# Fills, output projection and input split in smaller pieces at new steps, and the whole rotation on VectorE

## The chip, the core and the metric

The kernel runs on one core of a Trainium2 chip. The metric is the device time of one execution in microseconds (us). Five engines work side by side, each on its own list of instructions, and wait for one another on semaphores: TensorE (PE in the profile; PEld is its weight load), VectorE (DVE), ScalarE (ACT), GpSimd (POOL) and SyncE (SP), which issues most of the transfers between HBM and SBUF.

## The reference, cut to what matters

One transformer layer on 8 sequences ("batches") of 512 rows and 512 columns: differential attention, then a mixture of 8 experts, each with a residual and a layer norm.

```python
q, k, v = x @ Wq, x @ Wk, x @ Wv        # 16 heads of q, 4 of k and v, each two halves of 32 columns
q1, q2, k1, k2 = rope(...)              # o1 = x1*cos - x2*sin ; o2 = x1*sin + x2*cos
a1 = softmax(q1 @ k1.T * scale + mask); a2 = softmax(q2 @ k2.T * scale + mask)
out = (a1 - lam * a2) @ v
out = group_norm(out) * gn_w + gn_b     # mean and variance per head over all 512 rows
x1 = layernorm(x + out * (1 - LAMBDA_INIT) @ Wo)
# then: router, the best 2 of 8 experts for each row, silu(x@wg)*(x@wu)@wd, weighted sum, residual, layernorm
```

## The kernel before

The program has three parts: the attention of all batches, the experts, and the combination of their rows. The change touches the attention alone.

**The steps.** A batch is 48 steps: 4 groups of kv heads, each of 12 units. A unit is a tile of 128 query rows (tile 0 to 3) with two heads (tiles 0 and 1) or one head (tiles 2 and 3). In step s, TensorE computes the scores of unit s (`S<-kT,qT` and the mask), transposes the mixed probabilities of unit s-3 (`PTp<-ident,mixed`), and in some steps multiplies by the values (`O<-probsT,vals`). VectorE takes the row maximum of unit s (`neg_max`), inverts the sums of unit s-1 (`rsum`), mixes the two halves of unit s-2 (`mixed`) and computes the ratio of unit s-1 (`rho`). ScalarE copies the transposed probabilities of unit s-3 and takes the exponentials of unit s (`expd`). S has two buffers, so the scores of step s+1 wait for the exponentials of step s-1. The steps here are counted from the start of `neg_max`.

**The fills.** Beside its steps every batch projects 12 groups of 128 columns (`SEQ`: 8 of q, 2 of k, 2 of v), the first 7 for itself and the last 5 for the next batch. One such group is a fill: 12 matmuls (24 narrower ones for v) into `prep`. `STARTS` gives the step of a fill; half of it runs at the end of that step, half early in the next. For q and k a fill is followed by the rotation: VectorE reads `prep` and writes `turned` (times cos) and `swapped` (neighbours exchanged) one step after the start (`rotate`, L858 to L864), GpSimd multiplies `swapped` by sin and adds it to `turned` (`rope`, L486 to L492), VectorE rounds `turned` to the high part two steps later (`high_part`, L871), and GpSimd subtracts that for the low part (`low_part`, L494 to L498). SyncE stores both parts and loads them again in the layout of the scores (`spread`).

**The tail.** While batch b runs its steps, the tail of batch b-1 runs in them: statistics of the context (`chunk_stats`), group norm factors, 8 normalisations on ScalarE (`norm`, two in each of steps 12 to 15), 32 output projections on TensorE (`oproj`, two in each of steps 16 to 31), the residual and its statistics (`resid`), layer norm, transposition, router logits and the choice of experts. `TAIL_PE` and the tables `mine` of the engines give the steps. The single PSUM bank `tail` passes from task to task.

**The input.** After fill 6 SyncE loads x of the next batch, transposed, into `xl`; ScalarE rounds it to `xh` in step 31 (2048 columns at once), VectorE replaces `xl` by the remainder in step 32, and fill 7 waits for that in step 33.

The order on each engine is written out by hand in those tables; there is no scheduler. A waiting instruction holds everything behind it on its engine. Batches 1 to 6 run in a loop of two bodies; batch 0 has no tail, batch 7 only 7 fills, and its own tail comes after it, alone.

Of the kernel before, what the change touches and what calls it, by code (L numbers as in the profile page):

```python
# [21 lines left out]
F32 = mybir.dt.float32  # L22
# [51 lines left out]
TAIL_PE = {9: [("gn", 0)]}  # L74
OP0 = 16
for _i in range(NT):
    for _q in range(4):
        TAIL_PE[OP0 + 4 * _i + _q] = [("oproj", _i, _q)]
for _i in range(NT):
    TAIL_PE[OP0 + 19 + _i] = [("xT", _i)]  # L80
TAIL_PE[OP0 + 23] = [("logits", 0, 0)]
TAIL_PE[OP0 + 24] = [("logits", 0, 1)]
TAIL_PE[OP0 + 26] = [("rank", 0)]
# [56 lines left out]
def attention_block(nc, x, xT_d, wT_d, wv_d, wo_d, lam_d, gnw_d, gnb_d, gate_d, rope_d,  # L140
                    ident_d, identb_d, maskb_d, tri_d, avg_d, small_d, x1_dram, xs_dram, wsplit_dram, parts_dram, xint_dram,
                    ident, ones, slots, wts, msum):
    with ExitStack() as ctx:
# [232 lines left out]

        def fills(s, last, lag):

            for start, idx in STARTS.items():
                if start == s - lag and not (last and idx >= THIS_BATCH):  # L380
                    yield idx
# [96 lines left out]
        def _(pool):  # L478
# [15 lines left out]
            def low_part(n, r2):  # L494

                pool.wait_ge(hi_done, n + 1)
                nc.gpsimd.tensor_tensor(parts[r2][:, 1, :], turned[:], parts[r2][:, 0, :].bitcast(F32),  # L497
                                        ALU.subtract).then_inc(lo_done, 1)  # L498

# [17 lines left out]
            def body(b, first, second, last):  # L517
                for s, kv, u in steps(b, first, last):
                    for idx in fills(s, last, 1):
                        if SEQ[idx][0] != "v":  # L520
                            rope(group_no(b, idx), fill_no(b, idx), SEQ[idx][0])
                    for idx in fills(s, last, 3):
                        if SEQ[idx][0] != "v":
                            low_part(group_no(b, idx), half(b, idx))
# [21 lines left out]
            pool.wait_ge(consts_in, 16 * NCONST)  # L546
            for i in range(LEAD - 2):
                rope(i, i + 1, HEAD[i][0])
                low_part(i, i % 2)
# [12 lines left out]
        def _(pe):  # L562
            def fill_part(kind, j, part, w, count):

                if part == 0:
                    at_least(pe, prep_out, count - 1)
                if kind == "v":
                    here = slice((2 * j + part) * P, (2 * j + part + 1) * P)
                    o = prep[:, part * KV * HD:(part + 1) * KV * HD]
                    for c in range(DC):  # L570
                        nc.tensor.matmul(o, xh[:, c, here], wv[:, c, 0, :], start=(c == 0), stop=False)
                        nc.tensor.matmul(o, xh[:, c, here], wv[:, c, 1, :], start=False, stop=False)
                        mm = nc.tensor.matmul(o, xl[:, c, here], wv[:, c, 0, :], start=False, stop=(c == DC - 1))
                else:
                    for c in range(2 * part, 2 * part + 2):
                        nc.tensor.matmul(prep[:], w[:, c, 0, :], xh[:, c, :], start=(c == 0), stop=False)  # L576
                        nc.tensor.matmul(prep[:], w[:, c, 0, :], xl[:, c, :], start=False, stop=False)  # L577
                        mm = nc.tensor.matmul(prep[:], w[:, c, 1, :], xh[:, c, :], start=False, stop=(c == DC - 1))  # L578
# [1165 lines left out]
```

## Time and profile before

| | us |
|---|---|
| three timed runs | 2266.3, 2272.6, 2272.9 (median 2272.6) |
| the profiled execution: its own time | 2265.9 |
| its span in the profile | 2264.1 |
| before the first step of batch 0 | 57.6 |
| batch 0 | 172.8 |
| batches 1 to 6, from 230.4 to 1339.4 | 1109.0, or 184.8 each |
| batch 7 and the start of its tail, to 1512 | 172.6 |
| rest of that tail, to about 1570 | 58 |
| experts and combination | 694 |

The times of the batches are those between the first `neg_max` of one and of the next in the trace. The busy time of an engine in the profile counts instructions that take longer because they are held up, or because TensorE's clock is low; the granted clock stands beside it as a share of 2.4 GHz, and 0.5 is 1.2 GHz.

### The profile page before, as it was taken

The numbers are of one execution on the slowest core, as the hardware profiler recorded it, in microseconds if no ns is written. First come the engines' busy times: TensorE is split into PE (matmuls) and PEld (weight loads), VectorE is DVE, ScalarE is ACT, GpSimd is POOL, SyncE is SP. The second block draws the span as 40 slices with busy tenths as digits, with TensorE's granted clock in tenths as the row PEclk, the third lists the DMA queues.
The fourth block names the chain that finished last, engine by engine and source line by source line (L and its number), as shares of the span: only waits on it lengthen the run. The fifth ranks groups of instructions, "written<-read, shape, count | busy, mean of one in ns | idle before, by whom it ended". The sixth has DMA issues, their size and how long they took to land. (4 is left out here: it accounts for less than half of the span.)

```text
span 2264.1 us, 37174 instructions
## 1 busy us (share of the span) xinstructions
PE 1808.6 (80%) x9826; PEld 1336.3 (59%) x9827; DVE 1458.3 (64%) x3278; ACT 1129.6 (50%) x3263; POOL 614.6 (27%) x504
## 2 busy tenths in 40 slices
PE   3678898898889879879888888967099999999700
PEld 3455555656655755655655564544099999999600
DVE  2588867878788788787787878751333333333366
ACT  1466756667566575676667766661122222222133
POOL 2222312412231242241232223110542222200165
PEclk7788898899889889799989989988599999999855
DMA  7855534545454463453545455320543333223288
GB/s 262 282 139 152 145 99 140 178 112 149 134 166 120 126 200 114 124 174 103 159 151 147 129 152 168 75 75 19 181 146 112 112 114 120 74 83 98 73 269 269
DMA packets 142837, 319.51 MB, mean 141 GB/s; under 512 B 16704, under 2 KB 19264, under 8 KB 140512
## 3 DMA queue, kind: packets, MB, share of 16 engines
q1 hardware_dynamic: 113280, 241.84, 37.8%
q0 software_dynamic: 14432, 48.64, 6.4%
q10 hardware_dynamic: 14976, 27.27, 3.2%
q8 instruction: 66, 1.08, 0.2%
q14 instruction: 83, 0.68, 0.1%
HBM read 215.97 MB, written 109.05 MB: 144 GB/s over the span
## 5 line engine op out<-in xcount | busy, mean ns | idle before, releaser
L735 ACT ACTIVATE expd<-S,neg_max 128x128 f32<-128x128 f32 (+3 forms) x1024 | 530.7, 534 | 158.7 <-DVE neg_max L878 156.2
L878 DVE TENSOR_REDUCE neg_max<-S 128x2 f32<-128x768 f32 (+3 forms) x384 | 399.7, 1041 | 278.9 <-PE S L598 277.5
L909 DVE SCALAR_TENSOR_TENSOR mixed<-expd,rho 128x384 f32<-128x384 f32 (+3 forms) x512 | 337.2, 678 | 0.3 <-issue 0.3
L747 ACT ACTIVATE probsT<-PTp 128x512 f32<-128x512 f32 (+2 forms) x384 | 203.7, 531 | 254.0 <-PE PTp L609 251.3
L490 POOL TENSOR_TENSOR swapped<-swapped,rope_t 128x512 f32<-128x512 f32 x80 | 103.3, 1291 | 767.2 <-DVE swapped L864 767.2
L594 PE MATMUL S<-kT,qT 128*128 128x256 f32 (+2 forms) x1024 | 285.8, 382 | 27.4 <-DMA qT<-parts_rows 13.4
L609 PE MATMUL PTp<-ident,mixed 128*128 128x128 f32 x1280 | 221.3, 290 | 102.3 <-DVE mixed L909 99.7
L644 PE MATMUL tail<-wo,ctxT 128*128 128x512 f32 x512 | 252.9, 622 | 24.9 <-ACT ctxT L779 22.2
L594 PEld LDWEIGHTS S<-kT,qT 128*128 128x128 f32 x1024 | 165.7, 199 | 127.5 <-issue 82.4
L1311 ACT ACTIVATE xT_hi<-xTp 128x512 fp32r<-128x512 f32 x72 | 43.1, 599 | 359.2 <-DVE yo L1487 348.9
L609 PEld LDWEIGHTS PTp<-ident,mixed 128*128 128x128 f32 x1280 | 145.3, 148 | 126.6 <-DVE mixed L909 123.5
L735 ACT ACTIVATION_READ_ACCUMULATOR expd<-S,neg_max 128x1 f32 x1024 | 215.3, 210 | 0.0
L625 PE MATMUL O<-probsT,vals 128*64 128x256 f32 x1280 | 202.0, 454 | 0.0
L576 PE MATMUL prep<-xh,wqk 128*128 128x512 f32 x308 | 155.0, 503 | 20.8 <-DVE xl L1070 12.9
L497 POOL TENSOR_TENSOR parts<-turned,parts 128x512 fp32r<-128x512 f32 x80 | 123.3, 1541 | 169.2 <-DVE parts L871 169.0
L895 DVE SCALAR_TENSOR_TENSOR rho<-sums,neg_lam,rsum 128x1 f32<-128x1 f32 (+1 forms) x384 | 154.3, 402 | 0.0
L644 PEld LDWEIGHTS tail<-wo,ctxT 128*128 128x128 f32 x512 | 93.0, 197 | 102.2 <-issue 89.3
L625 PEld LDWEIGHTS O<-probsT,vals 128*64 128x64 f32 x1280 | 94.0, 159 | 67.3 <-issue 47.3
L577 PE MATMUL prep<-xl,wqk 128*128 128x512 f32 x308 | 130.2, 423 | 0.0
L578 PE MATMUL prep<-xh,wqk 128*128 128x512 f32 x308 | 129.8, 421 | 0.0
L1487 DVE COPY yo<-Y 128x512 f32<-128x512 f32 x72 | 49.8, 692 | 122.3 <-PE Y L1431 122.3
L598 PE MATMUL S<-maskb,identb 128*128 128x128 bf16 (+1 forms) x768 | 128.3, 250 | 0.0
(206 smaller groups left out, 3631.1 us busy)
## 6 DMA issues: line engine op xcount, KB each, us to landing
qT<-parts_rows SPq DMA_DIRECT2D x256, 256.0 KB, 4.6
parts_rows<-parts SPq DMA_DIRECT2D x160, 256.0 KB, 2.0
wqk<-wqk_split SPq DMA_DIRECT2D x75, 512.0 KB, 5.2
xin<-expert_in_rows SPq DMA_DIRECT2D x72, 256.0 KB, 2.9
expert_out_rows<-yo ACTq DMA_DIRECT2D x72, 256.0 KB, 3.2
kT<-parts_rows SPq DMA_DIRECT2D x64, 256.0 KB, 4.3
x<-in_x SPq DMA_DIRECT2D x8, 1024.0 KB, 7.8
x_rows<-x SPq DMA_DIRECT2D x8, 1024.0 KB, 7.0
```

The source lines that it names most:

```text
L576: nc.tensor.matmul(prep[:], w[:, c, 0, :], xh[:, c, :], start=(c == 0), stop=False)
L577: nc.tensor.matmul(prep[:], w[:, c, 0, :], xl[:, c, :], start=False, stop=False)
L578: mm = nc.tensor.matmul(prep[:], w[:, c, 1, :], xh[:, c, :], start=False, stop=(c == DC - 1))
L594: nc.tensor.matmul(S[s % 2][:, k * slot:k * slot + w], qT[kv % 2][:, 2 * h + c, i * P:(i + 1) * P], kT[kv][:, c, 0:w], start=(k % per_bank ...
L609: mm = nc.tensor.transpose(PTp[:, o:o + P], mixed[sl % 3][:, a * 256 + j * P:a * 256 + (j + 1) * P], ident[:])
L625: mm = nc.tensor.matmul(O[half * HD:(half + 1) * HD, 0], vals[kv][:, j, :], probsT[i % 2][:, j, half], start=(j == 0), stop=(j == i), tile ...
L644: mm = nc.tensor.matmul(tail[:], ctxT[par][:, c, i * P:(i + 1) * P], wo[:, c, :], start=(c == 0), stop=(c == FC - 1))
L735: ex = nc.scalar.activation(expd[s % 3][:, k * slot:k * slot + w], S[s % 2][:, k * slot:k * slot + w], ACT.Exp, bias=neg_max[s % 3][:, k:k ...
L747: nc.scalar.activation(probsT[i % 2][:, 0:i + 1, half:half + n, pair, :].rearrange("p j a q -> p a j q"), PTp[:, 0:w].rearrange("p (a j q) ...
L878: nc.vector.tensor_reduce(neg_max[s % 3][:, 0:k], v, AX, ALU.max, negate=True).then_inc(max_ready, 1)
L895: nc.vector.scalar_tensor_tensor(out=rr[:, i, h0:h0 + nh], in0=L[:, i, 0, h0:h0 + nh], scalar=neg_lam[:, 0:1], in1=Q[:, i, 1, h0:h0 + nh], ...
L909: ins = nc.vector.scalar_tensor_tensor(out=mixed[sl % 3][:, a * 256:a * 256 + w], in0=e2, scalar=rr[:, i, h:h + 1], in1=e1, op0=ALU.mult, ...
```

## The change

It has five parts.

1. **Fills in quarters.** `STARTS` gives way to `FILL_STEPS`, which names a step for each of the 4 pieces of a fill. A piece of a q or k fill is 3 matmuls; a v fill still has two pieces (at the entries 0 and 2).
2. **Rotation and split.** The two operations of `rope` go from GpSimd to VectorE (`turn`), one step after `rotate`. The rounding to the high part goes from VectorE to ScalarE (`high_part`), the low part from GpSimd to VectorE (`low_part`). GpSimd keeps the copies of v and the scatter of rows.
3. **Tail at new steps.** The output projection has one pair of matmuls in each of 16 steps named by `OPROJ` (14 to 33) instead of 16 in a row. The normalisations are one a step from step 12, and each signals, so that the first tile's projection waits for two at a time. The residual is in two tasks in successive steps (`add`, `spread`), the choice of experts in four, the statistics of the context have a step for each chunk (`CHUNK_STEPS`).
4. **Input in quarters.** ScalarE rounds x in steps 27 to 30 instead of 31, VectorE subtracts in steps 28 to 31 instead of 32, and fill 7 starts in step 29 instead of 33 and waits for one quarter at a time.
5. The layer norm of the tail moves from step 32 to step 34, the transpositions from 35 to 38 to 37 to 40, the logits from 39 and 40 to 41 and 42.

```diff
-STARTS = {0: 0, 4: 1, 8: 2, 12: 3, 16: 4, 24: 5, 27: 6, 33: 7, 36: 8, 39: 9, 42: 10, 44: 11}
+FILL_STEPS = [
+    (1, 1, 2, 2),
+    (4, 4, 4, 5),
...
+    (44, 44, 45, 45),
+]
-X_ROUND, X_LOW = 31, 32
+X_ROUND = 27
+OPROJ = [14, 17, 18, 20, 21, 22, 23, 25, 26, 27, 28, 29, 30, 31, 32, 33]
+CHUNK_STEPS = [18, 40, 37, 39, 48, 48, 54, 55]
+NORM0 = 12
+DONE = OPROJ[-1]
...
-            def rope(n, fill, kind):
-
-                sin = rope_t[:, 1 if kind == "q" else 3, :]
-                pool.wait_ge(prep_out, fill)
-                nc.gpsimd.tensor_tensor(swapped[:], swapped[:], sin, ALU.mult).then_inc(rope_step, 1)
-                pool.wait_ge(rope_step, n + 1)
-                nc.gpsimd.tensor_tensor(turned[:], turned[:], swapped[:], ALU.add).then_inc(rope_done, 1)
...
                 elif kind == "oproj":
                     i, q = task[1], task[2]
+                    if i == 0:
+                        pe.wait_ge(norm_ready, b * FC + 2 * q + 2)
                     if q == 0:
-                        pe.wait_ge(norm_ready, b + 1)
                         tail_bank_free(pe, b, "oproj", i)
...
+            def high_part(n, r2, total):
+
+                at_least(act, stacked[r2], total)
+                apart(act)
+                act.wait_ge(rope_done, n + 1)
+                nc.scalar.activation(parts[r2][:, 0, :], turned[:], ACT.Copy).then_inc(hi_done, 1)
...
-                nc.vector.tensor_copy(parts[r2][:, 0, :], turned[:]).then_inc(hi_done, 1)
+            def turn(n, fill, kind):
+
+                sin = rope_t[:, 1 if kind == "q" else 3, :]
+                dve.wait_ge(prep_out, fill)
+                nc.vector.tensor_tensor(swapped[:], swapped[:], sin, ALU.mult).then_inc(rope_step, 1)
+                dve.wait_ge(rope_step, n + 1)
+                nc.vector.tensor_tensor(turned[:], turned[:], swapped[:], ALU.add).then_inc(rope_done, 1)
+
+            def low_part(n, r2):
+
+                dve.wait_ge(hi_done, n + 1)
+                nc.vector.tensor_tensor(parts[r2][:, 1, :], turned[:], parts[r2][:, 0, :].bitcast(F32),
+                                        ALU.subtract).then_inc(lo_done, 1)
...
-                    if s == X_LOW and not last:
-                        low_x(b + 1, xl[:].bitcast(F32))
+                    if X_ROUND < s <= X_ROUND + DC and not last:
+                        low_x(b + 1, s - X_ROUND - 1, xl[:, s - X_ROUND - 1, :].bitcast(F32))
```

TensorE, a middle batch, the first output projection of the tail. Before, it stands in step 16 behind the wait for all 8 normalisations (`norm_ready`), with half of fill 4 behind it (`tail<-wo,ctxT` is the projection, `prep<-xh,wqk` the fill):

```order
L609 MATMUL PTp<-ident,mixed 128x128 [waits pT_out,mix_ready]
L609 MATMUL PTp<-ident,mixed 128x128
L351 ISA [waits norm_ready]
L644 MATMUL tail<-wo,ctxT 128x512 [waits tail_dve]
L644 MATMUL tail<-wo,ctxT 128x512
L690 REGISTER_ALU
L299 REGISTER_ALU [waits wqk_in0]
```

After, it stands in step 14, and the scores of step 15 follow it:

```order
L610 MATMUL PTp<-ident,mixed 128x128 [waits pT_out,mix_ready]
L610 MATMUL PTp<-ident,mixed 128x128 x3
L642 ISA
L365 ISA [waits norm_ready]
L646 MATMUL tail<-wo,ctxT 128x512 [waits tail_dve]
L646 MATMUL tail<-wo,ctxT 128x512
L313 REGISTER_ALU
L595 MATMUL S<-kT,qT 128x256 [waits exp_done]
```

The pair of projections moved two steps ahead and lost the half fill behind it; its wait is now for 2 of the 8 normalisations.

VectorE, a middle batch, step 17. Before, it holds the rotation of fill 4:

```order
L878 TENSOR_REDUCE neg_max<-S 128x2 [waits scores_ready]
L886 RECIPROCAL rsum<-sums 128x2 [waits exp_done]
L909 SCALAR_TENSOR_TENSOR mixed<-expd,rho 128x256 [waits pT_full,rho_step]
L909 SCALAR_TENSOR_TENSOR mixed<-expd,rho 128x256
L895 SCALAR_TENSOR_TENSOR rho<-sums,neg_lam,rsum 128x1 [waits rsum_step]
L860 REGISTER_ALU
L863 TENSOR_TENSOR turned<-prep,rope_t 128x512 [waits lo_done,prep_full]
L864 STREAM_SHUFFLE swapped<-prep 128x512
```

After, fill 4 is rotated in step 16, and step 17 holds the two operations that came from GpSimd:

```order
L902 TENSOR_REDUCE neg_max<-S 128x2 [waits scores_ready]
L910 RECIPROCAL rsum<-sums 128x2 [waits exp_done]
L933 SCALAR_TENSOR_TENSOR mixed<-expd,rho 128x256 [waits pT_full,rho_step]
L933 SCALAR_TENSOR_TENSOR mixed<-expd,rho 128x256
L919 SCALAR_TENSOR_TENSOR rho<-sums,neg_lam,rsum 128x1 [waits rsum_step]
L887 TENSOR_TENSOR swapped<-swapped,rope_t 128x512 [waits prep_out]
L888 REGISTER_ALU
L889 TENSOR_TENSOR turned<-turned,swapped 128x512 [waits rope_step]
```

Two operations of 512 columns stand behind `rho` here, and a third, the low part, two steps later; before there was the cast alone.

## Rows read from the trace of the kernel before

**Rows 1.** Windows by stage: length, busy us (instructions) of each engine, clock, DMA share, GB/s.
```profile
57.60:230.40 172.80, 128.52 (x717) 89.08 (x717) 132.83 (x266) 103.71 (x334) 43.67 (x33) 0.84 0.64 185
602.40:788.10 185.70, 163.23 (x871) 110.30 (x870) 147.40 (x334) 121.38 (x362) 51.87 (x43) 0.89 0.50 141
1339.40:1512.00 172.60, 145.85 (x782) 93.42 (x780) 134.15 (x322) 118.20 (x360) 45.02 (x38) 0.90 0.40 116
```
**Rows 2.** Windows in batch 3: steps 6; 16; 23 and 24; 39.
```profile
621.40:625.70 4.30, 1.43 (x11) 0.86 (x9) 4.30 (x7) 2.28 (x6) 4.03 (x4) 0.95 0.82 206
656.90:664.60 7.70, 5.80 (x19) 3.26 (x18) 2.41 (x7) 3.65 (x11) 0.00 (x0) 0.78 0.62 138
684.70:693.70 9.00, 9.00 (x50) 5.83 (x49) 5.52 (x13) 4.51 (x16) 0.00 (x0) 1.00 0.01 3
746.80:756.90 10.10, 9.83 (x49) 7.23 (x49) 3.23 (x8) 3.53 (x14) 1.38 (x1) 0.66 0.84 217
```
**Rows 3.** Waits of TensorE in batch 3: total us, times, longest.
```profile
PE PTp L609 <- DVE mixed L909: 11.0, 10, 2.3
PE tail L644 <- ACT ctxT L779: 1.9, 1, 1.9
PE prep L576 <- DVE xl L1070: 1.9, 1, 1.9
```
**Rows 4.** Groups by form on VectorE, 57 to 1512: count, busy us, mean ns, idle before.
```profile
L895 DVE SCALAR_TENSOR_TENSOR rho<-sums,neg_lam,rsum 128x1 f32<-128x1 f32 x255 | 126.5, 496 | 0.0
L909 DVE SCALAR_TENSOR_TENSOR mixed<-expd,rho 128x128 f32<-128x128 f32 x128 | 101.1, 829 | 0.3 <-issue 0.3
```
**Rows 5.** Line 895 in the whole trace: duration ns min/median/max.
```profile
L895 DVE SCALAR_TENSOR_TENSOR rho<-sums,neg_lam,rsum x384: 202/214/1255, 61.0 to 1512.3; 128x1 f32<-128x1 f32 x128, 128x2 f32<-128x2 f32 x64
```
**Rows 6.** Timeline, VectorE, batch 3: start us, duration us.
```profile
627.71 1.22 DVE L895 SCALAR_TENSOR_TENSOR rho<-sums,neg_lam,rsum 128x1 f32<-128x1 f32 x1
...
699.17 0.81 DVE L909 SCALAR_TENSOR_TENSOR mixed<-expd,rho 128x128 f32<-128x128 f32 x2
```
**Rows 7.** Timeline, GpSimd, batch 3.
```profile
627.29 1.62 POOL L497 TENSOR_TENSOR parts<-turned,parts 128x512 fp32r<-128x512 f32 x1 [0.31 <-DVE parts L871]
```
**Rows 8.** Groups on VectorE and ScalarE before batch 0.
```profile
L1085 DVE TENSOR_TENSOR kT<-ctxT,kT 128x512 fp32r<-128x512 f32 x4 | 2.6, 683 | 0.0
L848 ACT ACTIVATE kT<-ctxT 128x512 fp32r<-128x512 f32 x4 | 2.3, 618 | 10.0 <-PE prep L578 10.0
```
**Rows 9.** Timeline, VectorE, step 42 of batch 3: the cast.
```profile
767.74 0.42 DVE L871 CAST parts<-turned 128x512 fp32r<-128x512 f32 x1
```
**Rows 10.** Timeline, VectorE, step 40 of batch 3: start to start of 512 columns.
```profile
758.76 0.69 DVE L863 TENSOR_TENSOR turned<-prep,rope_t 128x512 f32<-128x512 f32 x1
759.37 0.02 DVE L864 LOAD_MASK_SELECT swapped<-prep  x1
```
**Rows 11.** Timeline, TensorE, batch 3: matmuls of a fill, clock full, then half.
```profile
692.34 0.39 PE L577 MATMUL prep<-xl,wqk 128*128 128x512 f32 x1
692.57 0.40 PE L578 MATMUL prep<-xh,wqk 128*128 128x512 f32 x1
...
751.27 0.63 PE L578 MATMUL prep<-xh,wqk 128*128 128x512 f32 x1
751.70 0.63 PE L576 MATMUL prep<-xh,wqk 128*128 128x512 f32 x1
```
**Rows 12.** Line 1070, VectorE, the input's remainder in one piece: ns min/median/max.
```profile
L1070 DVE TENSOR_TENSOR xl<-xl,xh x7: 2282/2285/2287, 179.7 to 1280.1; 128x2048 fp32r<-128x2048 f32 x7
```
**Rows 13.** Timeline, SyncE, batch 3: issue of the next input.
```profile
709.13 0.67 SPq L456 DMA_DIRECT2D xl<-xT_rows  x1
```
**Rows 14.** Transfers between 700 and 725: KB each, median us to landing.
```profile
xl<-xT_rows SPq DMA_DIRECT2D x1, 1024.0 KB, 8.8
```
**Rows 15.** Timeline, ScalarE: the input's rounding, and the norms after batch 7.
```profile
720.94 1.91 ACT L795 ACTIVATE xh<-xl 128x2048 fp32r<-128x2048 f32 x1
...
1523.61 5.74 ACT L779 ACTIVATE ctxT<-ctxT,gbi,gsc 128x512 f32<-128x512 f32 x8 [0.87 <-DVE gbi L960]
```

More of the change, by code:

```diff
@@ L375, in tile_no, with parts_of @@
             return ((b if s >= lag else b - 1) * KV + sl // NU) * NT + UNITS[sl % NU][0]
+        def parts_of(s, last, new):
+            for idx, at in enumerate(FILL_STEPS):
+                for c in range(DC):
+                    if at[c] == s and (at[0] == s) == new and not (last and idx >= THIS_BATCH):
+                        yield idx, c
         def fills(s, last, lag):
-            for start, idx in STARTS.items():
-                if start == s - lag and not (last and idx >= THIS_BATCH):
+            for idx, at in enumerate(FILL_STEPS):
+                if at[-1] == s - lag and not (last and idx >= THIS_BATCH):
                     yield idx
@@ L518, in body @@
                 for s, kv, u in steps(b, first, last):
[L519 to L524, printed above, removed]
                     if not first and not second:
@@ L680, in body @@
                         transposes(*lagged(b, s, LAG_T, first))
-                    for idx in fills(s, last, 1):
-                        fill_part(*SEQ[idx], 1, wqk[idx % 2][:], fill_no(b, idx))
+                    for idx, c in parts_of(s, last, False):
+                        project(b, first, idx, c)
                     if not first:
@@ L685, in body @@
                             tail_task(b - 1, 1 - par, task)
[L686 to L691 removed]
+                    for idx, c in parts_of(s, last, True):
+                        project(b, first, idx, c)
                     if (s - LAG_V) % NU in LAST_OF and lagged(b, s, LAG_V, first):
@@ L704, in end @@
                         tail_task(b - 1, (b - 1) % 2, task)
-            pe.wait_ge(xl_ready, 1)
             for i, (kind, j) in enumerate(HEAD):
                 pe.wait_ge(wl_ready, min(i, LEAD - 2) + 1)
-                for part in range(2):
-                    fill_part(kind, j, part, HOME.get((kind, j)), i + 1)
+                for c in range(DC):
+                    if i == 0:
+                        pe.wait_ge(xl_ready, c + 1)
+                    fill_part(kind, j, c, HOME.get((kind, j)), i + 1)
             pe.wait_ge(wl_ready, len(WORDER))
@@ L815, in body @@
                         widen(*lagged(b, s, 2, first), tile_no(b, s, 2))
-                    if s == X_ROUND and not last:
-                        round_x(b + 1, xl[:].bitcast(F32))
-                    for idx in fills(s, last, 1):
+                    if X_ROUND <= s < X_ROUND + DC and not last:
+                        round_x(b + 1, s - X_ROUND, xl[:, s - X_ROUND, :].bitcast(F32))
+                    for idx in fills(s, last, 2):
+                        if SEQ[idx][0] != "v":
+                            high_part(group_no(b, idx), half(b, idx), stack_total(b, idx) - GROUP_COUNT)
+                    for idx in fills(s, last, 0):
                         if SEQ[idx][0] == "v":
@@ L1028, in body @@
                     maxes(s, u)
-                    for idx in fills(s, last, 3):
-                        if SEQ[idx][0] != "v":
-                            high_part(group_no(b, idx), half(b, idx), stack_total(b, idx) - GROUP_COUNT)
                     if lagged(b, s, 1, first):
@@ L1075, in _ @@
             nc.vector.memset(eps_t[:], EPS).then_inc(lam_step, 1)
-            low_x(0, x1[:])
+            for c in range(DC):
+                low_x(0, c, x1[:, c, :])
             def low_w(i):
```

162 lines of the change are left out of this document (86 added, 76 removed).

## The prediction

> **What bounds the kernel now.** I read the page first, for its slices and its list of costly groups: the attention takes 1512 + 58 = 1570 of 2264 us and the change touches nothing behind it, so 694 us stand. Then the windows by stage [rows 1]. The reader is to see that no engine is full in batch 3: in 185.7 us TensorE is busy 163.2, VectorE 147.4, ScalarE 121.4. Two things inflate these numbers. TensorE's clock is granted at 0.89 in the mean, so 22% of the batch (0.11 / 0.5), some 41 us, runs at the lower level of 1.2 GHz, where a fill matmul follows the last one after 0.43 us and not after 0.23 [rows 11]; and VectorE's time holds time in which it was held up.
>
> Next, windows of single steps [rows 2]. In step 6 VectorE is busy 4.30 of 4.30 us and TensorE 1.43. In steps 23 and 24 TensorE is busy 9.00 of 9.00 and VectorE 5.52; in step 39 it is 9.83 against 3.23. With two buffers of S the engines can't drift more than about a step apart, so a step takes what its longer engine needs, and the longer engine changes from step to step. Last the waits: in batch 3 TensorE waits 11.0 us for `mixed`, 1.9 for the norms and 1.9 for the new input [rows 3], which is small beside 185.7.
>
> To turn this into a sum I took what each engine issues in each of the 48 steps, times the unblocked, full-clock duration of each kind of instruction, and added up the longer engine of each step. For steps 23 and 24 this gives 8.9 us, where the trace has 9.0 [rows 2]. TensorE comes to 140.5 us a batch and VectorE to 125.5. The sum of the longer engine is 165.0, and 172.8 with the held-up time of the next paragraph left in its steps (that batch 0 takes 172.8 as well is chance). The batches take 184.8, so 12.0 us are not in the sum: low clock where TensorE is the longer engine, the two waits of 1.9 us, and steps that don't fall in with their neighbours.
>
> **VectorE and GpSimd.** Line 895 computes one column per row. Its median is 214 ns, its longest 1255 [rows 5], and the form with one column has a mean of 496 over 255 [rows 4]. In batch 3 one lasts 1.22 us, from 627.71 to 628.93, and GpSimd's subtraction of the low part runs from 627.29 to 628.91 [rows 6, 7]. So it ended with GpSimd's instruction: it was held up, not slow. The mixing has the same: two of 128 columns take 0.81 us, 0.41 each, when nothing of GpSimd is beside them [rows 6], and the mean over 128 is 0.829 [rows 4]. That is 255 x (0.496 - 0.214) + 128 x (0.829 - 0.41) = 72 + 54 = 126 us, about 16 a batch over 8 batches; with the lesser forms I take 18. The Trainium skill, SBUF — State Buffer, section Who interferes with whom, says that a VectorE instruction with two inputs in SBUF and a GpSimd instruction share a port pair under an exclusive lock, so that one waits for the whole of the other. The trace agrees (1.22 us against 0.214).
>
> The change takes GpSimd's three operations per fill away, over 40 us of the 51.87 that it is busy in the batch [rows 1]; the copies of v stay. Of the 18 us some 8 lie in steps in which TensorE is the longer engine anyway, and 10 are exposed, as in step 6, where GpSimd was busy 4.03 of 4.30 us [rows 2].
>
> **What VectorE and ScalarE get.** A fill of q or k gives VectorE three operations of 512 columns with both inputs in SBUF. The nearest row is 683 ns [rows 8]; one that reads `prep` has 0.69 and 0.61 from start to start [rows 10]. The cast of 0.42 goes [rows 9]. That is 3 x 0.68 - 0.42 = 1.62 us a fill, 16.2 a batch with 10 such fills; the second operation waits for the first, 0.1 each, 1.0. The bounds are 3 x 0.61 - 0.42 = 1.41 and 3 x 0.83 - 0.42 = 2.07 (0.83 if some are still held up as the mixing was), 14 to 21 a batch. ScalarE gets the rounding, 0.62 [rows 8], 6.2 a batch, to 127.6 of 175 or more; it stays the third engine.
>
> **Steps.** With fills in quarters, projections that no longer stand beside half a fill, and the rotations at other steps, I made the same sum for the order after. Step 39 goes from TensorE 6.5 and VectorE 2.2 to 3.8 and 3.6; step 16 from 3.8 to 2.8 on TensorE while VectorE rises from 2.2 to 4.0; step 27 from 6.4 to 5.05 on TensorE; VectorE has 5.6 before and 2.8 after in step 40, 5.4 and 1.9 in step 42. TensorE's total is still 140.5, VectorE's is 140.8 (125.5 + 16.2 less roundings of the sum). The longer engine of each step adds up to 169.4, against 172.8: of the 16.2 us added about 10 are paid for by the end of the held-up time, the rest by the better mix. If neighbours can even out in pairs of steps, the sums without held-up time are 165.1 before and 157.5 after.
>
> **The 12.0 us that remain.** The norm wait goes: the first projection waits for two of eight, not all, and stands later than their end. The input wait becomes one for a quarter. That is 3.8 at most. The low clock follows stretches in which TensorE did little: the granted clock is 0.66 in step 39, where TensorE was busy nearly throughout, and 0.78 in step 16, behind a stretch of waiting, and 1.00 in steps 23 and 24 [rows 2]. Pieces that keep TensorE busier between such stretches should give back part. I take half of the 12.0 as left, 6.0; bounds are 0 and 12.
>
> One wait may be new. The input is rounded from step 27, four steps earlier. Its transfer is issued at 709.13 [rows 13], lands after 8.8 us [rows 14], at 718, and is used at 720.94 [rows 15], a slack of 3. After, SyncE issues it behind the stores of fill 6, whose low part now ends in step 24. By my sum that is 6.7 us past the start of that step, so it lands at 15.4, where ScalarE wants it at 13.3. If ScalarE waits, its exponentials behind it wait too, and so do TensorE's scores: 0 to 2.1 us a batch, in 7 batches. I take it as hidden by a buffer of S in the forecast, 1 us inside the 6.0.
>
> The input's remainder, 2.285 us in one piece [rows 12], becomes four of 0.683 [rows 8], 2.73: +0.45 a batch, in the sum. The Trainium skill, VectorE: DVE Perf Modes, section The TRN2 errata, speaks against the change here: each instruction pays a fixed cost, so many small tiles cost more. By its 2291 and 691 ns for 2048 and 512 columns, four pieces cost 0.47 more, an estimate from its figures; the rows say the same, and 7 x 0.45 = 3 us is the most it takes back.
>
> **Sum.** A middle batch: 169.4 + 6.0 = 175.4, against 184.8, so -9.4, and six give -56. Batch 0 has no tail, and its clock is lower (0.84 [rows 1]): -8. Batch 7 has seven fills: -7. Ahead of batch 0 three rotations are done on VectorE instead of GpSimd, in a chain, and the low parts end sooner: -2.5. After batch 7 the first projection waits for two norms and not for the row of eight, 5.74 us [rows 15], so about -4.3. Together -78: the profiled execution, 2265.9, becomes 2188. The median of the runs shown is 2272.6, 6.7 above it; the lowest of them is 2266.3. I say 2190. The forecast's own range, with 0 to 9 of the residual left and 14 to 21 added on VectorE, is 2155 to 2225.
>
> **Rivals.** *The residual stays.* The 12.0 us are clock and bad mixing that move elsewhere. Then a batch gains 3.4 from the sum alone: 6 x 3.4 + 6 + 7 = 33, 2237. For it: the mean clock hardly differs between stages (0.84 to 0.90 [rows 1]) though their work differs. Against it: two of its parts, 1.9 each, are waits that the change takes away [rows 3].
>
> *Neighbours even out.* The pairs of steps fall from 165.1 to 157.5, and with four pieces to a fill the residual mostly goes as well. Then a batch takes about 166: 6 x 19 + 36 = 150 less, 2119 or so. For it: TensorE waits 11.0 us for `mixed` in 10 places [rows 3], a sign of uneven steps. Against it: VectorE and TensorE would both be busy 85% of such a batch (141 / 166).
>
> *VectorE becomes the bound; slower.* Its place is steps 5 to 11 and 33 to 36, where VectorE has 3.7 to 4.1 us after the change and TensorE 0.9 to 3. If all that is added is exposed there and in the steps like them, 16.2 + 1.0 less the 10.5 recovered is 6.5 a batch, x 8 = 52, less the 6.8 at both ends: 2265.9 + 45 = 2311. It decides from the point at which VectorE is busy over 90% of the window of a batch. Against it: before, TensorE was busy 163.23 us and VectorE 147.40 [rows 1], and after VectorE is still at 141, as it loses as much held-up time as it gains work.
>
> *Nothing shows.* Gains and losses cancel, 2265 to 2279. A measurement of this kernel can tell a change from none at about 0.3%, 7 us, so this is its no change. The 9.4 us of a middle batch would have to be off by over 8, and in every one.
>
> **How the numbers follow.** I give 0.55 to the forecast, 0.20 to the residual that stays, 0.13 to evening out, 0.07 to VectorE as the bound, 0.05 to nothing. The time is that of the likeliest, 2190. The range of 2130 to 2258 takes in the forecast's own, the whole of the first rival and the half of the second. Faster by over 0.3% is 0.55 + 0.20 + 0.13 = 0.88, within it 0.05, slower 0.07.
>
> **What would show it.** The longest `rho` falls from 1.2 us to about 0.25 and the mean of the 128-column mixing to 0.41; if not, the held-up time had another cause. VectorE's busy time per middle batch is near 141 to 145, GpSimd's about 10. A middle batch takes about 175 us; the mean clock is 0.90 or above. TensorE's waits for the norms and for `xl` are gone. A wait of ScalarE for the transfer of `xl` in step 27, with a length of 2 us or more, would show the new wait. The sum is wrong if the steps do not take their longer engine: if batch 3 has TensorE and VectorE both idle for more than a few us. The forecast is wrong if the mean clock falls below 0.85, as the 6.0 us rest on it.

## The result and the profile after

The changed kernel takes 2142.1 us (median of 4 runs, 2141.2 to 2142.7), against 2270.0 of the kernel before on the same chips. The ratio is 0.9437, with a 95% interval of 0.9419 to 0.9455: 128 us less, where 83 were forecast from the median shown. 2142 lies in the stated range of 2130 to 2258, but below the forecast's own range of 2155 to 2225: it is inside only because the range also took in half of the second rival. The span of the profiled execution falls from 2264.1 to 2139.4 us, by 124.7. By stage, between the same instructions as in the table of before:

| | before | after | change | forecast |
|---|---|---|---|---|
| before the first step | 57.6 | 56.7 | -0.9 | -2.5 |
| batch 0 | 172.8 | 162.1 | -10.7 | -8 |
| batches 1 to 6, each | 184.8 | 168.1 | -16.7 | -9.4 |
| batch 7, to its last `neg_max` | 169.4 | 160.4 | -9.0 | -7 |
| from there to the first router logit | 65.3 | 64.5 | -0.8 | -4.3 |
| experts and combination | 690.0 | 686.9 | -3.1 | 0 |

So 44 us of the miss lie in the six middle batches. (The last row is 687 to 697 in the profiles of all the kernels here, whatever was changed in the attention. That is why the experiments below are compared by their middle batches. These come from one execution of each kernel, and single batches in it differ by up to 8 us, so a difference of a us or two in their mean is weak evidence.)

The windows by stage, batch 0, batch 3 and batch 7, to be held against [rows 1]:

```profile
56.70:218.80 162.10, 120.56 (x716) 85.44 (x715) 126.34 (x286) 106.43 (x347) 1.51 (x3) 0.88 0.68 197
556.80:723.90 167.10, 148.78 (x858) 101.45 (x858) 142.42 (x357) 125.26 (x373) 8.85 (x12) 0.96 0.55 155
1227.70:1388.10 160.40, 141.08 (x770) 93.05 (x772) 128.55 (x332) 120.28 (x364) 8.40 (x9) 0.93 0.39 112
```

In batch 3 the mean clock is 0.96, not 0.89; TensorE is busy 148.8 us with the work that took 163.2; VectorE has more instructions (357, not 334) in less time (142.4, not 147.4); GpSimd has 8.9 us.

The held-up time is gone. By form on VectorE, from 57 to 1512, and line 919 (895 of before) in the whole trace, for [rows 4, 5]:

```profile
L919 DVE SCALAR_TENSOR_TENSOR rho<-sums,neg_lam,rsum 128x1 f32<-128x1 f32 x256 | 55.6, 217 | 0.0
L933 DVE SCALAR_TENSOR_TENSOR mixed<-expd,rho 128x128 f32<-128x128 f32 x128 | 37.5, 335 | 0.0
```

```profile
L919 DVE SCALAR_TENSOR_TENSOR rho<-sums,neg_lam,rsum x384: 201/214/355, 59.1 to 1391.6; 128x1 f32<-128x1 f32 x128, 128x2 f32<-128x2 f32 x64
```

The median of `rho` is still 214 ns, but the mean is 217, not 496, and the longest 355 ns, not 1255. The mixing of 128 columns has a mean of 335 ns, not 829.

TensorE's waits in batch 3, for [rows 3]:

```profile
PE PTp L610 <- DVE mixed L933: 5.2, 6, 2.0
PE tail L646 <- ACT ctxT L786: 2.4, 2, 1.8
...
PE tail L646 <- DVE x L989: 1.1, 1, 1.1
```

The wait for `mixed` halves, and the one for the new input has no row any more. The wait for the norms is still there, 2.4 us in two places instead of 1.9 in one.

Last, four windows that the explanation needs. First those of before: step 7, which followed the idle step 6 of [rows 2], and steps 38 to 43, a stretch around step 39 of [rows 2].

```profile
625.70:630.00 4.30, 3.98 (x15) 2.01 (x16) 4.18 (x17) 1.62 (x5) 3.66 (x4) 0.50 0.52 199
743.70:778.10 34.40, 30.04 (x163) 23.57 (x161) 22.12 (x66) 14.58 (x47) 8.10 (x6) 0.70 0.60 158
```

The same of after: step 6, step 7, and steps 38 to 43.

```profile
574.00:577.80 3.80, 1.25 (x6) 0.77 (x6) 3.77 (x10) 1.68 (x5) 0.00 (x0) 0.94 0.61 146
577.80:582.10 4.30, 3.99 (x15) 2.00 (x16) 2.26 (x6) 2.14 (x6) 0.00 (x0) 0.50 1.04 231
690.40:712.60 22.20, 20.27 (x162) 16.35 (x161) 17.87 (x53) 17.32 (x51) 0.00 (x0) 1.00 0.63 159
```

Steps 38 to 43 are where most of the time came from. TensorE runs about as many instructions (162 against 163) in 22.2 us at full clock, where they took 34.4 at 0.70. The work is not quite the same: half of fill 9, 6 matmuls of 512 columns, now stands in step 37, in front of them, and more of the tail's small ones stand here. In the mean over six batches it is 33.3 and 22.2 us, which is 11.1 of the 16.7 us of a batch, with 17.6 and 0 us of low clock. Step 7, on the other hand, is as long as before, and at the lower clock in both: TensorE was idle for most of step 6, since VectorE is the longer engine there.

### The profile page after: what moved, and what is told of

Its sections match the earlier page's. It is cut to its first block and busy times, and to the rows that moved or that the text cites. A ratio compares the mean times of both kernels' runs of the same rounds, so it can differ in the third digit from the quotient of the medians.

```text
span 2139.4 us, 37290 instructions
## 1 busy us (share of the span) xinstructions
PE 1730.7 (81%) x9826; PEld 1291.0 (60%) x9827; DVE 1424.2 (67%) x3462; ACT 1165.0 (54%) x3367; POOL 283.9 (13%) x264
## 5 line engine op out<-in xcount | busy, mean ns | idle before, releaser
L646 PE MATMUL tail<-wo,ctxT 128*128 128x512 f32 x512 | 244.2, 604 | 25.8 <-ACT ctxT L786 15.6
L933 DVE SCALAR_TENSOR_TENSOR mixed<-expd,rho 128x384 f32<-128x384 f32 (+3 forms) x512 | 262.7, 534 | 0.1
L741 ACT ACTIVATION_READ_ACCUMULATOR expd<-S,neg_max 128x1 f32 x1024 | 210.5, 206 | 0.0
L626 PE MATMUL O<-probsT,vals 128*64 128x256 f32 x1280 | 179.1, 412 | 0.0
L505 POOL COPY vals<-vnext 128x256 f32<-128x256 f32 x32 | 17.2, 567 | 1148.4 <-ACT vnext L729 1109.4
L577 PE MATMUL prep<-xh,wqk 128*128 128x512 f32 x308 | 148.0, 481 | 12.5 <-DMA wqk<-wqk_split 12.5
L579 PE MATMUL prep<-xh,wqk 128*128 128x512 f32 x308 | 126.4, 410 | 0.0
L626 PEld LDWEIGHTS O<-probsT,vals 128*64 128x64 f32 x1280 | 84.9, 144 | 54.8 <-issue 29.5
L1499 DVE TENSOR_TENSOR xT_lo<-xTp,xT_hi 128x512 fp32r<-128x512 f32 x72 | 49.8, 692 | 100.9 <-ACT xT_hi L1344 100.9
L1442 PE MATMUL G<-w_hi,xT_hi 128*128 x288 | 100.3, 348 | 2.4 <-issue 0.8
```

The costliest lines, as they stand in the source:

```text
L626: mm = nc.tensor.matmul(O[half * HD:(half + 1) * HD, 0], vals[kv][:, j, :], probsT[i % 2][:, j, half], start=(j == 0), stop=(j == i), tile ...
L646: mm = nc.tensor.matmul(tail[:], ctxT[par][:, c, i * P:(i + 1) * P], wo[:, c, :], start=(c == 0), stop=(c == FC - 1))
L741: ex = nc.scalar.activation(expd[s % 3][:, k * slot:k * slot + w], S[s % 2][:, k * slot:k * slot + w], ACT.Exp, bias=neg_max[s % 3][:, k:k ...
L933: ins = nc.vector.scalar_tensor_tensor(out=mixed[sl % 3][:, a * 256:a * 256 + w], in0=e2, scalar=rr[:, i, h:h + 1], in1=e1, op0=ALU.mult, ...
```

## The experiments

Times are medians; the ratio is to the kernel before on the same chip, with its 95% interval. "Middle batch" is the mean over batches 1 to 6 of the profiled execution, and "low clock" the time in such a batch for which the granted clock is 0.5. The profiled execution is not always near the median: in e5 it is 13.8 us above it (2180.0), in e6 6.6 above, in e7 7.9 below (2122.4) and in e10 5.6 below.

| | us | ratio | middle batch | low clock |
|---|---|---|---|---|
| before | 2270.0 | 1 | 184.8 | 36.4 |
| after | 2142.1 | 0.9437 (0.9419 to 0.9455) | 168.1 | 11.9 |
| e1 | 2231.5 | 0.9851 (0.9805 to 0.9897) | 180.2 | 26.7 |
| e2 | 2134.2 | 0.9436 (0.9393 to 0.9479) | 166.4 | 6.8 |
| e3 | 2231.8 | 0.9857 (0.9815 to 0.9899) | 180.4 | 18.8 |
| e4 | 2188.9 | 0.9660 (0.9607 to 0.9713) | 172.5 | 6.8 |
| e5 | 2166.2 | 0.9531 (0.9493 to 0.9569) | 172.8 | 15.4 |
| e6 | 2151.2 | 0.9462 (0.9423 to 0.9501) | 169.3 | 12.5 |
| e7 | 2130.2 | 0.9387 (0.9353 to 0.9422) | 166.3 | 4.6 |
| e8 | 2143.7 | 0.9441 (0.9409 to 0.9473) | 168.3 | 10.8 |
| e9 | 2152.7 | 0.9481 (0.9432 to 0.9529) | 169.8 | 15.9 |
| e10 | 2129.1 | 0.9382 (0.9348 to 0.9417) | 165.6 | 2.8 |
| e11 | 2126.1 | 0.9350 (0.9311 to 0.9388) | 165.4 | 1.7 |

**e1: the kernel before, with only the rotation and the low part on VectorE.**

```diff
-                nc.gpsimd.tensor_tensor(swapped[:], swapped[:], sin, ALU.mult).then_inc(rope_step, 1)
...
+                nc.vector.tensor_tensor(swapped[:], swapped[:], sin, ALU.mult).then_inc(rope_step, 1)
...
+                    for idx in fills(s, last, 3):      # VectorE, behind ratios
+                            low_part(group_no(b, idx), half(b, idx))
+                    for idx in fills(s, last, 2):
+                            turn(group_no(b, idx), fill_no(b, idx), SEQ[idx][0])
```

> The kernel before with one thing changed: the two operations of the rotation and the low part run on VectorE (the rotation's in the step behind `rotate`), while fills, projections, norms and input stay in their old steps and the cast stays on VectorE. Theory A, that the new steps make the gain and the end of the held-up time only pays for what VectorE gets: VectorE loses 18 us of held-up time a batch and gains 20 us of work (3 x 0.68 a fill), so a batch changes by -2 to +5 us and the kernel takes 2255 to 2310. Theory B, that the lock between VectorE and GpSimd was the costly thing: most of the 128 us come with this part alone, 2150 to 2200.

Batch 3 and, in it, steps 38 to 43:

```profile
579.30:761.30 182.00, 160.31 (x870) 108.42 (x869) 146.19 (x363) 120.49 (x362) 8.25 (x12) 0.92 0.51 143
719.90:751.40 31.50, 28.03 (x162) 22.42 (x161) 21.63 (x72) 14.45 (x47) 0.00 (x0) 0.78 0.61 158
```

A middle batch gets 4.6 us shorter, and the kernel 1.5% faster. It lies between the two theories: the loss of VectorE's held-up time pays for all that VectorE gets (146.2 us busy against 147.4) and a little more, but most of the gain needs the new steps. Low clock falls by 9.7 us a batch as well, though nothing on TensorE was moved. Most of this gain stands in steps 38 to 43: 7.4 us less of low clock there (17.6 to 10.2 in the mean) and 3.6 us less of time (33.3 to 29.8), 0.48 for each.

**e2: the changed kernel, with rotation and low part back on GpSimd.**

```diff
-                nc.vector.tensor_tensor(swapped[:], swapped[:], sin, ALU.mult).then_inc(rope_step, 1)
...
+                nc.gpsimd.tensor_tensor(swapped[:], swapped[:], sin, ALU.mult).then_inc(rope_step, 1)
...
+                    for idx in fills(s, last, 0):      # GpSimd
+                            rope(group_no(b, idx), fill_no(b, idx), SEQ[idx][0])
+                    for idx in fills(s, last, 2):
+                            low_part(group_no(b, idx), half(b, idx))
```

> The changed kernel with the rotation's two operations and the low part back on GpSimd; all steps stay new, the rounding stays on ScalarE. Theory A: VectorE loses 20 us of work a batch and gets 18 us of held-up time back, of which some falls on steps where TensorE is longer; the new steps keep their gain, 2145 to 2185. Theory B: the lock takes back most of the gain, 2220 or more. One-column `rho` has again a longest of about 1.2 us under both.

Batch 3, and line 929 (`rho`) of this kernel:

```profile
557.80:722.20 164.40, 146.28 (x859) 99.20 (x858) 136.83 (x327) 124.76 (x372) 48.11 (x42) 0.98 0.56 158
```

```profile
L929 DVE SCALAR_TENSOR_TENSOR rho<-sums,neg_lam,rsum x384: 202/210/1253, 61.2 to 1381.0; 128x1 f32<-128x1 f32 x128, 128x2 f32<-128x2 f32 x64
```

VectorE is held up again, up to 1253 ns, and yet the kernel is as fast as the changed one (the intervals lie on each other; a middle batch is 1.7 us shorter, batch 0 4.4 longer, batch 7 6.6 shorter). So theory A holds, and more sharply than it was put (2134 is below its 2145 to 2185): beside the new steps, the part of the change that takes the rotation to VectorE is worth nothing that can be measured. Held-up time is about 11 us a batch here, counted over `rho` and `mixed` beyond their unblocked durations, against 18.4 before, and VectorE is spared about 20 us of work by it.

**e3: the kernel before, with TensorE kept busy.**

```diff
+                    if s in [2, 6, 7, 10, 14, 15, 32, 38]:
+                        at_least(pe, prep_out, ...)
+                        for _ in range(12):
+                            nc.tensor.matmul(prep[...], identb[:], maskb[...], start=True, stop=True)   # 256 columns
```

> The kernel before with work added and nothing taken away: in steps 2, 6, 7, 10, 14, 15, 32 and 38 TensorE runs 12 more matmuls of 256 columns into the free bank `prep`, whose result nobody reads (about 1.3 us a step at full clock), in steps in which it was busy 0.5 to 4 us and waited otherwise. Theory C, that the forecast missed the low clock: low-clock time falls from 27 to 41 us a batch to under 20, the steps with fills behind these gain, and the kernel gets faster in spite of 10 us more work a batch, 2190 to 2245. Theory D, that the missed gain is better mixing alone and the clock comes with it: the same or slower, 2268 to 2300.

```profile
586.90:765.70 178.80, 162.62 (x966) 113.50 (x965) 147.18 (x333) 120.86 (x362) 51.95 (x43) 0.95 0.52 146
```

96 matmuls were added to the batch (the trace has records of 95), nothing was taken away, and it is shorter. TensorE is busy as long as before (162.6 and 163.2 us) with more in it, as the mean clock is 0.95, not 0.89. This shows that low clock cost the kernel before time. 17.6 us less of it gave 4.4 us, 0.25 us for each, net of the work added. By the medians of the runs it is 33.6 us for 150 us less in the whole attention, 0.22. Only 1.7 of the 17.6 lie in steps 38 to 43, so this is the price of low clock elsewhere.

**e4: the changed kernel, all fills in halves at the steps of before** (so the input is rounded from step 30, and subtracted ahead of `rotate` in a step).

```diff
-    (1, 1, 2, 2), ... (37, 37, 38, 38), (40, 40, 42, 42),
+    (0, 0, 1, 1), ... (39, 39, 40, 40), (42, 42, 43, 43),
-X_ROUND = 27
+X_ROUND = 30
```

> The changed kernel with its fills in halves at the steps of before (each half in the step of the table and the next), the input rounded in steps 30 to 33; engines, projections, norms and the rest of the tail stay new. If the quarters at new steps carry the mixing, a batch gets 5 to 9 us longer and low-clock time rises again towards 30 us: 2180 to 2215. If the rest (engines, tail) carries it, 2142 to 2155.

ScalarE's wait in batch 3, in a row of the waits:

```profile
ACT xh L801 <- DMA xl<-xT_rows: 5.9, 1, 5.9
```

In the range, but low clock did not rise (6.8 us), against the expectation, and the kernel has a wait that I had not wanted. Hence e5. Most of the wait falls into step 31, which takes 7.2 us in the mean.

**e5: the same without that wait:** fills 5, 6 and 7 and the input stay at the new steps.

> The changed kernel with fills 0 to 4 and 8 to 11 in halves at the steps of before; fills 5, 6 and 7 and the input keep the new steps, so that ScalarE does not wait for the input's transfer, as it did 5.9 us a batch in the first test of halves. Theory E, that the quarters carry the mixing: a middle batch takes 172 to 176 us against 168.1, and the kernel 2175 or more. Theory F, that they are worth little and the first test measured the wait: 168 to 171, and the kernel 2142 to 2165, with batch 0 making up most of the difference.

Batch 3, and steps 38 to 43 in it:

```profile
566.80:737.90 171.10, 150.90 (x864) 101.52 (x862) 142.29 (x357) 124.92 (x373) 7.97 (x11) 0.96 0.54 151
700.10:726.40 26.30, 22.57 (x159) 17.89 (x159) 19.07 (x57) 18.67 (x54) 0.00 (x0) 0.94 0.41 114
```

By the profiled execution a middle batch takes 172.8 us, as theory E said: halves cost 4.7 us, 4.2 of them in steps 38 to 43 (26.4 in the mean, against 22.2). But that execution is the slowest of the four, 2180.0, and 9.8 us of it are in the experts and combination alone. The median, 2166.2, is under E's 2175 and just over F's 2165. If the last stage is left as in the changed kernel, the 24.1 us between the medians leave 3.8 a middle batch. So the halves cost some 4 us, and neither theory's numbers hold in full. My sum over the longer engines gives 169.7 for these steps and 169.4 for the changed kernel: it does not see this.

Nor was e4's wait free. A middle batch is as long there (172.5), but e4 is 23 us slower by the medians and the ratios' intervals don't meet (from 0.9607, and up to 0.9569); batch 0 has 7.6 of these. Step 31 of batch 3, with the wait (e4) and without it (e5):

```profile
683.10:690.70 7.60, 4.49 (x23) 2.23 (x22) 2.87 (x7) 2.36 (x6) 0.00 (x0) 0.99 0.65 230
675.40:679.30 3.90, 3.90 (x22) 1.92 (x21) 2.29 (x6) 2.11 (x6) 0.00 (x0) 1.00 0.00 0
```

With nearly as many instructions the step is 3.7 us longer; e4 makes up for it in other steps, with fills 5, 6 and 7 in halves too and 8.6 us less of low clock.

**e6: the changed kernel, output projection in 16 successive steps.**

```diff
-OPROJ = [14, 17, 18, 20, 21, 22, 23, 25, 26, 27, 28, 29, 30, 31, 32, 33]
+OPROJ = list(range(18, 34))
```

> The changed kernel with the output projection in 16 successive steps, 18 to 33, instead of 16 chosen steps from 14 to 33; the norms, the fills and all that follows step 33 stay. The residual follows the projections by itself (steps 21, 25, 29, 33). The sum over the longer engine of each step is 172.9 against 169.4, so if the steps decide, a middle batch gets 3.5 us longer and the kernel takes 2160 to 2175. If neighbouring steps even out anyway, the sums over pairs differ by 2.4 and the kernel takes 2145 to 2158.

A middle batch gets 1.2 us longer, by the sum it should be 3.5. With a ratio of 0.9462 the interval overlaps that of the changed kernel, and the kernel's time is in the range for steps that even out. Whether the 1.2 us are real can't be told; the 3.5 are not there, so neighbouring steps even out.

**e7: the changed kernel, TensorE kept busy in three steps.**

```diff
+                    if s in [6, 11, 36]:
+                        ... 8 matmuls of 256 columns into prep
```

> The changed kernel with work added: 8 matmuls of 256 columns into the free bank `prep` in steps 6, 11 and 36, whose result nobody reads. There the list has 0.9, 2.9 and 1.2 us for TensorE and the low clock follows, 10 to 14 us a batch. Theory C (low clock costs about a quarter of its time, as the same test on the kernel before gave: 17 us less of it, 4.4 us a batch gained): low-clock time falls to under 5 us and a middle batch gains 2 us, 2120 to 2138. Theory D: no gain, 2140 to 2150, since VectorE is the longer engine there.

Steps 6 and 7 of batch 3, as above for the changed kernel:

```profile
566.50:570.30 3.80, 2.66 (x18) 1.88 (x18) 3.77 (x9) 1.69 (x5) 0.00 (x0) 1.00 0.48 127
570.30:572.90 2.60, 2.27 (x16) 1.31 (x17) 2.27 (x7) 1.62 (x5) 0.00 (x0) 1.00 1.03 243
```

Step 6 takes 3.8 us as before, with more work on TensorE. Step 7 has full clock and falls from 4.3 to 2.6 us. In the mean over the batches step 7 goes from 4.36 to 2.60, step 37 from 4.28 to 3.18, step 12 from 2.71 to 2.04. Theory C holds, and by the profiled execution with the same price: 7.3 us less of low clock gives 1.8 us, 0.25 for each. That execution is the fastest of the four; by the medians it is 11.8 us for 68 us less in the whole attention, 0.17. The kernel is faster than the changed one by the ratios, 0.9387 against 0.9437, but narrowly: the intervals overlap by a hair (up to 0.9422, and from 0.9419). All its four times lie below the four of the changed kernel.

**e8: e2 with two quarters moved.**

```diff
-    (7, 8, 9, 10),
+    (6, 8, 9, 10),
-    (37, 37, 38, 38),
+    (36, 37, 38, 38),
```

> A try at a faster one: the new steps with the rotation and the low part on GpSimd, which gave 166.4 us for a middle batch, and two quarters of fills moved into the steps in which TensorE has least: the first of fill 2 from step 7 to 6, the first of fill 9 from 37 to 36. The work is the same. If the low clock behind steps 6 and 36 goes, a middle batch gains 1 to 2 us more: 2118 to 2130. If held-up VectorE sets these steps, 2130 to 2140.

Batch 3, and step 39 in it:

```profile
558.70:726.80 168.10, 150.31 (x864) 101.44 (x863) 138.13 (x327) 125.78 (x374) 48.45 (x42) 0.96 0.55 154
692.90:699.60 6.70, 4.84 (x26) 2.86 (x27) 3.64 (x7) 5.70 (x18) 2.54 (x2) 0.75 0.81 175
```

A miss: no faster than e2 (ratios 0.9441 and 0.9436), with a middle batch 1.9 us longer. Step 37 gained 1.7 us (3.94 to 2.29 in the mean), but 5.7 us of low clock came up in steps 39 to 42, where e2 has none and TensorE has more work: step 39 went from 4.90 to 6.70 us in the mean. That it is the quarter missing from step 37 that let the clock fall there is my reading, and was not tried by itself.

**e9: the changed kernel with only fills 9 and 10 in halves.**

```diff
-    (37, 37, 38, 38),
-    (40, 40, 42, 42),
+    (39, 39, 40, 40),
+    (42, 42, 43, 43),
```

> The changed kernel with only fills 9 and 10 in halves at the steps of before (39 and 40, 42 and 43, instead of 37 and 38, 40 and 42). Theory G, that the gain beyond the sum over longer engines came from few places where a whole half fill, the tail's wait for ScalarE and low clock met, above all steps 38 to 43: these six steps grow from 22.2 us by more than the 2.8 us that the sum gives (21.2 to 23.9), to 26 or more, and a middle batch takes 171 to 173. Theory H, that only the sum counts: 25 us in these steps and 170 to 171 a batch.

Steps 38 to 43 of batch 3, and step 39 alone:

```profile
695.10:719.10 24.00, 21.37 (x161) 16.91 (x160) 17.65 (x53) 18.21 (x53) 0.00 (x0) 0.97 0.44 128
698.00:704.90 6.90, 4.96 (x37) 3.42 (x35) 2.51 (x7) 5.90 (x19) 0.00 (x0) 1.00 0.70 181
```

The six steps take 25.1 us in the mean over the batches, 2.9 more than after, where the sum gives 2.8. This is theory H's 25 and not theory G's 26 or more. Step 39 is at full clock in this batch and still takes 6.9 us. A middle batch, 169.8, is just under both theories. So two halves alone don't bring back what before lost there, and my picture that they did has fallen.

**e10 and e11: two tries at the fastest.** e10 is e2 with e7's matmuls. e11 is e7 with the same matmuls in six more steps of batch 0 alone.

```diff
+                    if s in [6, 11, 36] or (first and s in [3, 22, 25, 28, 33, 39]):
```

> The rotation and low part on GpSimd with the new steps, and the 8 matmuls of 256 columns in steps 6, 11 and 36 whose result nobody reads. If the low clock is what both share, each with about 2 us of gain a middle batch, it takes 165 us and the kernel 2122 to 2130. If the gains overlap, since the version on GpSimd had only 6.8 us of low clock a batch left, 2128 to 2138.

> The changed kernel with the added matmuls of 256 columns in steps 6, 11 and 36 and, in batch 0 alone, also in steps 3, 22, 25, 28, 33 and 39. Batch 0 had 31.7 us of low clock left with the first three. At a quarter of a us for each us of low clock that goes, batch 0 falls from 158.3 to about 155 and the kernel takes 2122 to 2130; middle batches stay at 166.3. If the work added costs more than the clock gives, 2131 to 2136.

Batch 0 of e11:

```profile
56.20:214.10 157.90, 120.85 (x789) 86.85 (x789) 126.38 (x287) 106.28 (x347) 1.51 (x3) 0.94 0.70 203
```

e10 takes 165.6 us a middle batch, 0.7 less than e7: the two gains overlap for the most part. e11 has the lowest time, 2126.1 and a ratio of 0.9350, beating both kernels. But its reason was wrong: batch 0 has 13 us less of low clock than in e7 (18.6 against 31.7) and is no shorter (157.9 against 158.3). In batch 0 TensorE waits for transfers (12.5 us once for `wqk` after the change); that a low clock beside such a wait costs nothing would explain it, but was not tried by itself. The intervals of e7 and e11 overlap, so a step between the two isn't shown.

## Why the prediction was right, and where it was mis-sized

**The sum over longer engines.** It gave -3.4 a batch (172.8 to 169.4). It is near where the clock is full: in steps 18 to 32 it says 55.3 us for the changed kernel and 58.3 for the one before, and the batches take 54.9 and 56.9. It is a rough tool for a comparison, though: it misses by 3.5 to 4.4 us in e5 and by 2.3 in e6, with opposite signs. So the 3.4 of it can't be trusted to better than some 4 us.

**The residual, the step that failed.** "I take half of the 12.0 as left, 6.0; bounds are 0 and 12." What was left is -1.3 (168.1 less 169.4), just beyond the lower bound. By stretches of steps, the same sum (with held-up time in its steps) and the mean over six batches:

| steps | before: sum, measured | after: sum, measured |
|---|---|---|
| 0 to 11 | 39.5, 41.4 | 39.3, 39.5 |
| 12 to 17 | 23.0, 25.5 | 20.9, 20.6 |
| 18 to 32 | 58.3, 56.9 | 55.3, 54.9 |
| 33 to 37 | 15.0, 17.1 | 19.8, 18.7 |
| 38 to 43 | 27.3, 33.3 | 21.2, 22.2 |
| 44 to 47 | 9.7, 10.7 | 13.0, 12.2 |

Half of the 12.0 stood in six steps, 38 to 43, in which TensorE was the longer engine and its clock 0.70, and 2.5 in steps 12 to 17, with the norm wait and step 16 at 0.78. I had read both windows [rows 2] and still spread the residual evenly. With the change 5.0 of these 6.0 went. The low clock accounts for a good part of the 13.3 us by which the residual fell. It fell by 24.5 us a batch, 17.6 of them in steps 38 to 43. At the 0.17 to 0.25 of e3 and e7 all of it is worth 4 to 6 us. But in steps 38 to 43 TensorE is the longer engine, and there e1 has 0.48 for each us; a fill matmul loses 0.20 of 0.43 us, about as much [rows 11]. At that price the 17.6 are worth some 8 us, an estimate that is more than the 5.0 that went there. The waits that I had taken off give little: they were 3.8 us, and the one for the norms stayed, 2.4, so 1.4. That leaves 2 to 8 us of the 13.3 that I can't assign. Evening out is part of it, as e6 shows, and so may be TensorE's wait for VectorE's `ctxT`, which fell from 5.0 us in batch 3, 2.7 of them in steps 38 to 43, to 1.3:

```profile
PE O L622 <- DVE ctxT L917: 5.0, 2, 2.7
PE O L623 <- DVE ctxT L941: 1.3, 1, 1.3
```

Which part of the new steps freed steps 38 to 43 stays open. Of the 11.1 us there, the rotation's place alone gave 3.6 on the old steps (e1) and nothing on the new ones (e2: 22.2), and the halves took back 4.2 at most (e5). The tail's transpositions and logits, moved by the fifth part of the change, stand in the same steps and were not tried alone.

**Held-up VectorE.** The mechanism is right: `rho` and the mixing fell to their unblocked durations. For the mixing that is 0.335 us and not the 0.41 of the sum. The pair of 0.81 us at 699.17 [rows 6] was read as having nothing of GpSimd beside it, but it had:

```profile
698.30 1.26 POOL L492 TENSOR_TENSOR turned<-turned,swapped 128x512 f32<-128x512 f32 x1
```

The Trainium skill, SBUF — State Buffer, section Who interferes with whom, names the exclusive lock, and e2 agrees, as the same instruction lasts up to 1253 ns once GpSimd rotates again. My balance, some 10 us recovered against 16.2 added, was right in that the two nearly cancel: -4.6 a batch with the old steps (e1), +1.7 with the new ones (e2 against after). "The rest by the better mix" was the larger part.

**VectorE's and ScalarE's new work.** 142.4 us and 125.3 us in batch 3, where 141 to 145 and 127.6 were forecast. The input's remainder in four pieces:

```profile
L1101 DVE TENSOR_TENSOR xl<-xl,xh x28: 681/684/692, 164.2 to 1169.9; 128x512 fp32r<-128x512 f32 x28
```

4 x 0.684 = 2.74 us against 2.285 in one [rows 12], +0.45 as worked out. The Trainium skill's rule against small tiles (VectorE: DVE Perf Modes, The TRN2 errata) holds by its size and doesn't decide: the four pieces lie in steps 28 to 31, and in two of these TensorE is clearly the longer engine by my sum (4.2 us against 3.2, and 3.9 against 2.2).

**The new wait for the input.** Expected at 0 to 2.1 us and hidden; the trace has one of 0.4 in step 27 of batch 3. That even a long one would be hidden is not so: with e4's, of 5.9, the step is 3.7 us longer than without (e5).

```profile
ACT xh L801 <- DMA xl<-xT_rows: 0.4, 1, 0.4
```

**The norm wait.** "The first projection waits for two of eight, not all, and stands later than their end" was wrong: it stands earlier, in step 14, while the norms now run one a step from 12. The wait stays, 2.4 us, and its longest is 1.8, against 1.9 before.

**The end tail.** I gave -4.3 and it was -0.8. On VectorE, after the last `neg_max` (at 1508.80) of before, and (at 1388.07) of after:

```profile
1517.99 0.42 DVE L917 TENSOR_TENSOR ctxT<-O,scale 128x256 f32<-128x256 f32 x1 [4.37 <-ACT scale L763]
1518.57 1.29 DVE L925 BATCH_NORM_STATS2 bn<-ctxT 128x6 f32<-128x512 f32 x2 [0.16 <-DVE ctxT L917]
```

```profile
1399.66 0.42 DVE L941 TENSOR_TENSOR ctxT<-O,scale 128x256 f32<-128x256 f32 x1 [6.78 <-ACT scale L769]
1400.00 2.46 DVE L948 BATCH_NORM_STATS2 bn<-ctxT 128x6 f32<-128x512 f32 x4
```

TensorE's projections before and after:

```profile
1529.41 9.02 PE L644 MATMUL tail<-wo,ctxT 128*128 128x512 f32 x16 [7.62 <-ACT ctxT L779]
```

```profile
1407.78 9.99 PE L646 MATMUL tail<-wo,ctxT 128*128 128x512 f32 x16 [3.39 <-ACT ctxT L786]
```

The wait for the norms did fall by 4.2 us (7.62 to 3.39). Three things take it back: the first tiles run at the pace of the norms (9.99 against 9.02), `CHUNK_STEPS` leaves four chunks of statistics for after the last step instead of two, 1.2 us, and the last context is ready 11.6 us behind the last `neg_max` instead of 9.2. The second stands in the diff, and I had not counted it.

**The rivals.** VectorE as the bound didn't happen: it is busy 85% of a middle batch, under the 90% from which it should decide. "Neighbours even out" put a batch at 166 and the kernel at 2119: the middle batch, 168.1, is nearer to it than to my 175.4, and the time, 2142, stands between the two, nearer to 2119. So the middle batches went the way of this rival, to which I gave 0.13. Three of the rivals' numbers don't follow from their terms: from 2265.9, the residual that stays comes to 2233 and not 2237, and evening out to 2116 and not 2119; VectorE's 16.2 + 1.0 - 10.5 is 6.7 and not 6.5. None of this matters here.

## What to carry to other kernels

Look at the granted clock in the windows of the steps in which TensorE is the longer engine, and put the residual of a sum there, not everywhere: here six such steps held half of it, and they got shorter by 11.1 us where the sum gave 6.1. When a lock between two engines goes at the price of work on the engine that was held up, it may be worth little, as here; measure it apart from the reordering that comes with it. A step in which TensorE idles can be followed by a slow one (step 7 here); if there is real work that fits, move it, but see which step it leaves short (e8).

## What the runs showed of the hardware

Matmuls that nobody needs made two kernels faster: 96 a batch the kernel before by 1.4% (e3), 24 a batch the changed one by 0.5% (e7, with intervals that overlap by a hair). The step behind an idle one went from 4.3 us at a clock of 0.50 to 2.6 at 1.00. And e1 had 9.7 us a batch less of low clock though no instruction of TensorE was moved; only GpSimd's rotation had gone to VectorE.
